# Full attention loops: the rows of minus the maximum turned for two groups at once, and one slot for two projections

## The reference, cut to what matters

```python
def attention(x):                       # L0_attn, 16 heads of 8 channels, no mask
    q, k, v = split(x @ w_qkv + b_qkv)
    p = softmax(q @ k.T / sqrt(8))      # 2048 queries x 2048 keys, for each head
    return (p @ v) @ w_out + b_out

def routed_attention(x):                # L2_ffn: 8 experts, the best 2 of them for each token
    gate, chosen = top_k(router(x), 2)
    y = 0
    for e in range(8):                  # queries: the tokens that chose e; keys and values: all tokens
        a = softmax((x @ qW[e]) @ (x @ kW[e]).T / sqrt(8)) @ (x @ vW[e])
        y += gate[e] * (a @ oW[e])
    return y
```

## Time and profile before

| | |
|---|---|
| median of three runs | 3931.2 us (3928.16 to 3935.24) |
| the profiled execution, its own time | 3919.58 us |
| its span | 3917.9 us |
| TensorE matmul busy | 3201.4 us (82%), 54200 instructions |
| VectorE busy | 2926.3 us (75%), 3610 |
| ScalarE busy | 2528.6 us (65%), 4873 |
| GpSimd busy | 601.5 us (15%), 1574 |
| mean granted TensorE clock | 0.907 |
| L0_attn loop | about 80 to 715 us |
| causal loop | about 800 to 1250 us |
| routed loop | about 2294 to 3705 us |

### The profile page before, as it was taken

One profiled execution on the slowest core, in us unless ns is written; L12 is line 12 of the kernel. 1 busy time (PEld: TensorE's weight loads), 2 busy tenths in 40 slices (PEclk: granted clock), 3 DMA queues, 4 the chain that ended last, 5 costly groups with the idle time before them and its releaser, 6 DMA issues. The chain is left out here.

```text
span 3917.9 us, 127868 instructions
## 1 busy us (share of the span) xinstructions
PE 3201.4 (82%) x54200; PEld 2084.5 (53%) x54200; DVE 2926.3 (75%) x3610; ACT 2528.6 (65%) x4873; POOL 601.5 (15%) x1574
## 2 busy tenths in 40 slices
PE   2999999479998897565764449999999999999638
PEld 1666666335555674122433326666666666666424
DVE  5999999458884113898353359999999999999653
ACT  1899999447777333432211229999999999999622
POOL 0010000011100000464004011111111111111220
PEclk7999999779999898899866769999999999999859
DMA  5000000310000000540008755555454545455410
GB/s 117 9 8 9 7 10 5 84 34 11 9 7 3 22 16 9 173 144 31 5 5 129 234 152 123 130 124 134 117 135 117 135 116 135 117 135 117 108 32 11
DMA packets 198682, 295.81 MB, mean 76 GB/s; under 512 B 93668, under 2 KB 128042, under 8 KB 197062
## 3 DMA queue, kind: packets, MB, share of 16 engines
q1 hardware_dynamic: 191478, 276.38, 28.3%
q10 hardware_dynamic: 2048, 6.29, 0.9%
q0 software_dynamic: 4592, 5.05, 0.6%
HBM read 225.51 MB, written 53.39 MB: 71 GB/s over the span
## 5 line engine op out<-in xcount | busy, mean ns | idle before, releaser
L890 ACT ACTIVATE channels_qk<-psum 128x512 f32<-128x512 f32 x3842 | 2061.1, 595 | 263.7 <-PE psum L716 189.6
L958 DVE TENSOR_REDUCE l2f_chunk_max<-psum 128x2 f32<-128x1024 f32 x1144 | 1324.8, 1217 | 76.3 <-PE psum L691 67.8
L958 DVE TENSOR_REDUCE chunk_max<-psum 128x2 f32<-128x1024 f32 (+2 forms) x832 | 916.8, 1156 | 112.2 <-PE psum L691 62.6
L691 PE MATMUL psum<-l2f_k_parts,l2f_q_parts 48*128 48x512 bf16 x2288 | 697.0, 388 | 42.5 <-DVE l2f_chunk_max L958 31.2
L737 PE MATMUL psum<-channels_qk,l2f_v_and_ones 128*9 128x128 f32 x17920 | 698.5, 274 | 14.1 <-issue 14.1
L716 PE MATMUL psum<-l2f_q_parts,l2f_k_parts 51*128 51x128 bf16 x8968 | 706.5, 218 | 0.4 <-ACT l2f_minus_max_rows L938 0.4
L691 PE MATMUL psum<-k_parts,q_parts 48*128 48x512 bf16 (+3 forms) x1664 | 424.5, 382 | 103.2 <-DMA q_parts<-q_rows_dram 73.6
L716 PEld LDWEIGHTS psum<-l2f_q_parts,l2f_k_parts 51*128 51x128 bf16 x8968 | 482.4, 94 | 30.7 <-ACT channels_qk L890 23.2
L737 PE MATMUL psum<-channels_qk,v_and_ones 128*9 128x128 f32 x12544 | 492.7, 275 | 0.6 <-ACT channels_qk L890 0.5
L716 PE MATMUL psum<-q_parts,k_parts 51*128 51x128 bf16 x6272 | 432.5, 218 | 31.1 <-DMA q_parts<-minus_max_rows 10.5
L737 PEld LDWEIGHTS psum<-channels_qk,l2f_v_and_ones 128*9 128x9 f32 x17920 | 386.0, 90 | 121.3 <-issue 23.7
(11 more groups left out here) (476 smaller groups left out, 3178.0 us busy)
## 6 DMA issues: line engine op xcount, KB each, us to landing
l2f_k_parts<-l2f_k_parts_dram SPq DMA_DIRECT2D x588, 192.0 KB, 3.8
l2f_v_and_ones<-expert_v_dram SPq DMA_DIRECT2D x144, 288.0 KB, 4.3
l1a_bc_rows<-ssm_rows_dram SPq DMA_DIRECT2D x32, 512.0 KB, 4.7
expert_v_dram<-l2f_v_and_ones SPq DMA_DIRECT2D x8, 1152.0 KB, 4.3
channels_qk<-ssm_rows_dram SPq DMA_DIRECT2D x16, 512.0 KB
l2f_q_parts<-l2f_gathered_q_parts SPq DMA_DIRECT2D x444, 16.0 KB
k_parts<-k_rows_dram ACTq DMA_DIRECT2D x32, 192.0 KB, 7.6
q_parts<-q_rows_dram SPq DMA_DIRECT2D x64, 96.0 KB, 2.5
```

What stands on the lines that cost most here:

```text
L691: last = nc.tensor.matmul(c.ps[:, 2 * (n % 2) + j, 0:width], at.q[64 * j:64 * j + ROWS, tile % SLOTS, pair, :], kx(tile)[64 * j:64 * j + R ...
L890: nc.scalar.activation(at.prob[:, s % 4, j, 0:kts, :].rearrange("p k q -> p (k q)"), c.ps[:, ring.bank(i, n), 0:kts * 2 * P], ACT.Exp, sca ...
L958: v.tensor_reduce(at.mx[:, 4 * g + 2 * pp:4 * g + 2 * pp + 2, chunk], c.ps[:, 2 * (n % 2):2 * (n % 2) + 2, 0:span.width(tile, chunk)], X, ...
```

## The change

In the two full loops the rows of two groups (12 values for each of 128 queries and group) are turned by one transpose into 24 rows, copied by one ScalarE instruction, and loaded by four DMAs in a row. That happens after step 11 for groups 2 and 3 of this tile, and after step 27 for groups 0 and 1 of the next; the slots after steps 3 and 19 fall away. In the routed loop `q` and `proj` share one slot after step 20: two matmuls into two halves of one bank, then two ScalarE instructions. The queries of L0_attn for two tiles on are loaded after step 11 in place of step 3. Before the loop the rows of groups 0 and 1 are turned together, once that of group 1 is there. The causal loop is unchanged.

```diff
-        self.mrow = sb(ctx, "minus_max_rows", [12, 4, P], BF16)
+        self.mrow = sb(ctx, "minus_max_rows", [24, 4, P], BF16)
...
+    def turned_with(self, group):
+
+        return (group,) if self.span.causal else (group - 1, group) if group % 2 else ()
...
-            if self.routed or i + ahead < self.tiles:
+            if self.turned_with(group) and (self.routed or i + ahead < self.tiles):
                 names.append(f"rows{group}")
...
-        if self.routed and s in (14, 17):
-            names.append("turn" if s == 14 else "q")
-        if self.routed and i > 0 and s == 20:
-            names.append("proj")
+        if self.routed and s in (14, 20):
+            names.append("turn" if s == 14 else "q_proj")
...
             def load_max(g, tile):
+                first, column = (0, g) if span.causal else (12 * (g % 2), g // 2)
                 for j in range(2):
...
             def load_later_max(i, g):
                 group, ahead = ring.rows_in(g)
-                if exists(i + ahead):
+                if exists(i + ahead) and ring.turned_with(group):
                     sp.wait_ge(s2_read, ring.read_when(i, ring.place(i, f"rows{group}")))
-                    load_max(group, i + ahead)
+                    for turned in ring.turned_with(group):
+                        load_max(turned, i + ahead)
...
             for g in range(lead - ring.late):
-                sp.wait_ge(first_rows_copied, g + 1)
+                sp.wait_ge(first_rows_copied, g + 1 if span.causal else 1)
                 load_max(g, 0)
...
-            def turn_rows(g, bank):
-                return nc.tensor.transpose(c.ps[:, bank, :].bitcast(BF16)[0:12, 0:P],
-                                           at.mparts[:, g, :, :, :].rearrange("p j n a -> p (j n a)"), c.identb[:, :])
+            def turn_rows(groups, bank):
+                return nc.tensor.transpose(c.ps[:, bank, :].bitcast(BF16)[0:12 * len(groups), 0:P],
+                                           at.mparts[:, groups[0]:groups[-1] + 1, :, :, :].rearrange("p g j n a -> p (g j n a)"), c.identb[:, :])
...
-                elif name == "proj":
-                    project(i, n, ring.place(i, "turn"))
-                elif name == "q":
-                    project_q(i, n, ring.place(i, "turn"))
+                elif name == "q_proj":
+                    if i > 0:
+                        project(i, n, ring.place(i, "turn"))
+                    project_q(i, n, ring.place(i, "turn")).then_inc(s2_ready, 1)
```

More of the change, by code:

```diff
@@ L415, in attention_loop @@
     SLOTS = 3
+    FIRST_ROWS = lead - ring.late if span.causal else 1
     oT = c.ps[:, 7, :]
@@ L525, in tile_loads @@
                     load_later_max(i, g)
-                    if g == 0 and i + 2 < tiles:
+                    if g == (0 if span.causal else 1) and i + 2 < tiles:
                         load_q(i + 2)
@@ L545, in routed_loads @@
                     if g == 3 and i > 0:
-                        sp.wait_ge(s2_read, ring.read_when(i, ring.place(i, "proj")))
+                        sp.wait_ge(s2_read, ring.read_when(i, ring.place(i, "q_proj")))
                         sp.dma_start(routed.y_dram[i], routed.y[:, :]).then_inc(y_stored, 16)
@@ L655, in whole_tile @@
                         pool.wait_ge(q_loaded[(i + 1) % 2], ((i + 1) // 2 + 1) * QL)
-                        pool.wait_ge(s2_read, ring.read_when(i, ring.place(i, "q")))
+                        pool.wait_ge(s2_read, ring.read_when(i, ring.place(i, "q_proj")))
                         split_q()
@@ L763, in project_q @@
                 pe.wait_ge(w_q_loaded[i % 2], (i // 2 + 2) * 16)
-                nc.tensor.matmul(c.ps[:, ring.bank(i, n), 0:P], routed.w_q_now[:, i % 2, 0:P], routed.turned[:, 1, :],
-                                 start=True, stop=True).then_inc(s2_ready, 1)
+                return nc.tensor.matmul(c.ps[:, ring.bank(i, n), P:2 * P], routed.w_q_now[:, i % 2, 0:P], routed.turned[:, 1, :],
+                                        start=True, stop=True)
             def project(i, n, turned):
@@ L770, in project @@
                 pe.wait_ge(w_out_loaded, i * 16)
-                nc.tensor.matmul(c.ps[:, ring.bank(i, n), 0:P], routed.turned[:, 0, :], routed.w_out_now[:, :], start=True, stop=True).then_inc(s2_ready, 1)
+                return nc.tensor.matmul(c.ps[:, ring.bank(i, n), 0:P], routed.turned[:, 0, :], routed.w_out_now[:, :], start=True, stop=True)
             def side_work(i, g, name):
@@ L789, in side_work @@
                     pe.wait_ge(mparts_ready, (i + ahead) * G + (group + 1))
-                    turn_rows(group, ring.bank(i, n)).then_inc(s2_ready, 1)
+                    turn_rows(ring.turned_with(group), ring.bank(i, n)).then_inc(s2_ready, 1)
             def causal_tile(i):
@@ L860, in _ @@
                 if g > 0 and g - 1 < lead - ring.late:
-                    if routed and g > 1:
-                        pe.wait_ge(first_q_copied, 2)
-                    pe.wait_ge(mparts_ready, g)
-                    turn_rows(g - 1, ring.BANK0 + 3 - g).then_inc(first_rows_turned, 1)
-            pe.wait_ge(first_rows_copied, lead - ring.late)
+                    groups = ring.turned_with(g - 1)
+                    if groups:
+                        if routed:
+                            pe.wait_ge(first_q_copied, 2)
+                        pe.wait_ge(mparts_ready, g)
+                        turn_rows(groups, ring.BANK0 + 3 - g).then_inc(first_rows_turned, 1)
+            pe.wait_ge(first_rows_copied, FIRST_ROWS)
             second_pass(0, (0, 1), 0)
@@ L880, in _ @@
                 turn_heads(done, 3).then_inc(s2_ready, 1)
-                project(done, 4, 3)
+                project(done, 4, 3).then_inc(s2_ready, 1)
         @block.scalar
@@ L896, in copy_out_channels, with copy_rows @@
                 nc.scalar.activation(at.oTs[:, :], oT, ACT.Copy).then_inc(oT_copied, 1)
+            def copy_rows(group, bank):
+                rows, column = (12, group) if span.causal else (24, group // 2)
+                return nc.scalar.activation(at.mrow[0:rows, column, :], bank.bitcast(BF16)[0:rows, 0:P], ACT.Copy)
             def empty(name, i, n, heads=True, tokens=True):
@@ L936, in _ @@
             for g in range(lead - ring.late):
-                act.wait_ge(first_rows_turned, g + 1)
-                nc.scalar.activation(at.mrow[:, g, :], c.ps[:, ring.BANK0 + 2 - g, :].bitcast(BF16)[0:12, 0:P], ACT.Copy).then_inc(first_rows_copied, 1)
+                if ring.turned_with(g):
+                    act.wait_ge(first_rows_turned, g + 1 if span.causal else 1)
+                    copy_rows(g, c.ps[:, ring.BANK0 + 2 - g, :]).then_inc(first_rows_copied, 1)
             done = each_tile(act, whole_tile)
```

11 lines of the change are left out of this document (7 added, 4 removed).

## The result

The changed kernel takes 4011.1 us (median of four runs, 4006.28 to 4012.91) against 3930.6 us (3928.16 to 3935.24) of the kernel before: ratio 1.0199, 95% interval 1.0184 to 1.0213. It is slower by 80 us. The prediction said slower, at 3954 us; the loss is 3.5 times as large, and the time lies outside the range. All times and ratios here are of executions in the faster of two states of the chip; one execution of a later experiment, at 9803 us, was in the other and is left out.

What follows compares the result with a forecast made beforehand. Three engines nearly full in both full loops, so VectorE's idle time counts; -3.6 - 16.3 + 37.9 + 5.0 = +23.0 us on the profiled 3919.6 gives 3942.6, put on the median as 3954; range 3930 to 3974.

Steps and rivals of the forecast that it cites:

- (a): L0_attn: removing the rows slot before `out` gains 0.24 us in each of 15 tiles, 3.6 us.
- (b): Routed loop: fewer rows slots and joint `q` and `proj` slot gain 0.48 us a tile, 16.3 us in 34 tiles.
- (c): Routed loop, step 3: values issued 1.49 us later behind two extra row loads make TensorE wait, 37.9 us lost.
- (d): Routed loop: query parts, wanted at step 8, go out 1.49 us later; covered by step 3's wait, cost nothing.
- (e): Routed loop: group 0's rows load with 0.66 us margin, no cost; group 2's smaller margin left to a rival.
- third rival: Much slower: group 2's rows, behind keys after step 11, land late; 31 us on top, 3985 us, chance 0.07.
- forecast case: The main forecast, with values late at step 3 of the routed loop: 3954 us, chance 0.68.
- (f): Start of each full loop: the second pass waits 2.5 us for group 0's rows, 5.0 us lost in all.
- first rival: Faster: the extra issues cost the values nothing at step 3 of the routed loop; 3916 us, chance 0.12.
- The 50 ns per dispatch: SP queue: by this figure two more issues shift the values only 0.1 us; the prediction preferred the row's 1.49 us.

Runs made afterwards that it cites:

- g8_behind: Changed kernel, routed loop: last quarter of the values issued ahead of step 27's rows, one pair of keys behind step 11's rows; 3921.3 us, ratio 0.9981.
- e3_split: Changed kernel, routed loop: rows of the second of the two groups loaded behind the values, not ahead; 4052.6 us, 139.5 above the kernel before.

## Why the prediction was right in sign and wrong in size

- (a) L0_attn: right. The wait is 0.43 us in place of 0.70 (forecast 0.46), and from the first tile's `out` to the last one's the loop takes 553.7 us in place of 557.7 (forecast 3.6 less).
- (b) The routed slots: right to the size. The changed kernel has no quiet tile in this loop; g8_behind, with the same slots, has. In the one shown above VectorE waits 0.33 us at `out` and 0.29 at the joint slot (forecast 0.46 and 0.43), and three times 0.11 to 0.15 elsewhere, 1.03 us in all. Before it was 1.51 (the 1.37 and a wait of 0.14). So 0.48 us is gained, as forecast, though not where it was forecast. The length of the tile shows 0.43 of it, and 34 such would be 14.6 us (forecast 16.3).
- (c) Late values: the wait itself was right. 44.0 us where 4.1 were, so 39.9 against a forecast of 37.9. (One of the 8 waits of the earlier trace rows, 0.52 us at 3607.81, is not at step 3, so 7 tiles were late and not 8; that is worth half a microsecond.) The price of the wait was wrong. The step that failed is "26 tiles wait 1.49 - 0.5 = 1.0 us, and the 8 late ones wait 1.49 more: 26.0 + 11.9 = 37.9 us": it takes an engine that waited for one that goes on at its old pace. Lateness of 1.49 us alone cost 73.5 us, twice the term. Behind many waits of 0.65 us and more TensorE ran at its lower clock, which cost such a tile 1.2 to 2.6 us more, or gave its results late without a mark in the record (17 and 11 tiles of 33 in the changed kernel).
- (d) Query parts: at nothing, as forecast. That the wait at step 3 covers them is right too: without that wait TensorE waited for them, 2.2 us in g8_behind and 8.5 in e3_split.
- (e) and the third rival: I gave group 0 no cost and group 2 a chance of 0.07. Group 0 never waited. Group 2 did, 13.1 us at 15 waits, for the reason the rival names (the rows stand behind keys in one queue). It came beside the forecast case and not in place of it; I had treated them as exclusive. With the values in time it is the larger cost: 45 to 76 us of waiting.
- (f) Starts: TensorE waited 3.05 and 2.98 us for the first load (forecast 2.5 each), but undoing it gained nothing that could be measured.
- The range held bounds for the length of the wait, and none for what follows it. With 73.5 in place of 37.9 and 13.1 us for the rows, my sum is +72 where +80 was measured. Behind three of the waits for rows (1.3 to 1.4 us each) the trace of the changed kernel has a low clock again, so part of the other 8 us is what follows those waits; e3_split shows the same on a larger scale. No run splits it off exactly.
- The first rival (values hidden, 3916) is out: four small issues took 2.97 us, 0.74 each, and one added issue of this size in each tile cost 18 us.
- The 50 ns per dispatch, which the prediction took from the Trainium skill, "DMA: Bandwidth & Descriptors", section "Anatomy of one DMA — SWDGE (gpsimd) path", do not hold on SP's queue, by the same 0.74 us. That section is on DMAs issued by GpSimd, and no row here is of those.

## What to carry to other kernels

On a queue that issues without pause, a load that is moved ahead of another is a delay of it; ask for every load behind the new place what its slack is, and for the moved one what bytes stand ahead of it. An engine that is nearly full pays more for a wait of about 1 us than the wait, so price such a wait at one and a half to a little over two times its length (48 us for 31 of work, 73.5 for 40.4 of added waiting, 17.7 for 8.2), and one well under 0.65 us at its length or less. And when one wait is taken away, look for the one that it had been hiding: here moving the values alone left 62 us of the loss.

## What the hardware showed that was not expected

- TensorE's granted clock fell to the lower level behind single waits of 0.65 to 2.2 us, in 18 of 33 tiles with two extra loads, while waits just as long left it at 1.00 in others (1.19 and 1.24 us above). It cost 1.2 to 1.4 us of a 39 us tile in 12 of them and 2.3 to 2.6 in six.
- Work in place of idling kept the record at 1.00, yet results mostly came 0.8 to 1.1 us later than the rows say, in the kernels with late values and in those without. What this time is stays open.
- With the DMA engines full for 4 us (218 and 235 GB/s), TensorE stopped 1.8 us inside a run of matmuls that waits for nothing. All 30 such stops ended 1.3 to 1.8 us after a 16 KB packet of the instruction queue.
- A load of 1.5 KB takes SP 0.74 us to issue, twice as long as one of 288 KB (0.35).
